# Attention sums of a graph network on Trainium2: blocks of 13 nodes per step instead of 25, six steps' sums copied at once

## The reference

```python
def gatv2_layer(x, src, dst, Wl, bl, Wr, br, att, bias, n_nodes):
    C = att.shape[1]
    xl = (x @ Wl + bl).reshape(n_nodes, H, C)
    xr = (x @ Wr + br).reshape(n_nodes, H, C)
    e = jax.nn.leaky_relu(xl[src] + xr[dst], NEG_SLOPE)
    alpha = jnp.einsum('ehc,hc->eh', e, att)
    m = jax.ops.segment_max(alpha, dst, num_segments=n_nodes)
    m = jnp.where(jnp.isfinite(m), m, 0.0)
    a = jnp.exp(alpha - m[dst])
    denom = jax.ops.segment_sum(a, dst, num_segments=n_nodes)
    a = a / (denom[dst] + 1e-16)
    out = jax.ops.segment_sum(a[:, :, None] * xl[src], dst, num_segments=n_nodes)
    return out.mean(axis=1) + bias
...
h = jax.nn.relu(gatv2_layer(x, src, dst, W1l, b1l, W1r, b1r, att1, bias1, n))
h = jax.nn.relu(gatv2_layer(h, src, dst, W2l, b2l, W2r, b2r, att2, bias2, n))
return h @ Wfc + bfc
```

## Time and profile before

| | us |
|---|---|
| median of 3 runs | 6792.11 (6786.22 to 6797.61) |
| profiled execution | 6792.24 |
| its span | 6790.6 |
| TensorE busy (matmul) | 4317.3 (64%) |
| VectorE busy | 4718.2 (69%) |
| ScalarE busy | 2352.3 (35%) |
| GpSimd busy | 3732.1 (55%) |
| first layer's sums, first to last matmul | 4795.5 to 5106.1 |
| last matmul of the second layer's sums | 6664.5 |

### The profile page before, as it was taken

The page is one execution under the profiler, slowest core; times in us unless marked ns, Lnnn a source line. Parts: engine busy times, 40 slices in busy tenths (PEclk is TensorE's granted clock), DMA queues, the critical chain, the costliest instruction groups (busy, mean ns, idle before and its releaser), DMA issues. The chain is left out here.

```text
span 6790.6 us, 97826 instructions
## 1 busy us (share of the span) xinstructions
PE 4317.3 (64%) x25290; PEld 3565.7 (53%) x25291; DVE 4718.2 (69%) x7252; ACT 2352.3 (35%) x3587; POOL 3732.1 (55%) x4221
## 2 busy tenths in 40 slices
PE   5888889210168846666655656664697666665597
PEld 2788888210058846566653333333696333333496
DVE  4677777688721127777756988887675998887674
ACT  5555555116612216666641112111221112111121
POOL 3677777000200027777754777774655777775453
PEclk9555555555569878888877888887897888888796
DMA  8799898994478753343435777775664777776562
GB/s 325 239 264 261 262 267 259 240 258 156 166 289 304 270 183 113 129 140 113 151 87 131 191 201 202 201 201 141 138 142 123 195 200 202 201 201 165 119 144 63
DMA packets 1471918, 1296.05 MB, mean 191 GB/s; under 512 B 1257959, under 2 KB 1297403, under 8 KB 1458874
## 3 DMA queue, kind: packets, MB, share of 16 engines
q1 hardware_dynamic: 902214, 671.42, 32.9%
q0 software_dynamic: 167008, 441.69, 24.2%
q10 hardware_dynamic: 402580, 181.62, 9.7%
HBM read 942.07 MB, written 351.27 MB: 190 GB/s over the span
## 5 line engine op out<-in xcount | busy, mean ns | idle before, releaser
L2519 POOL DMA_INDIRECT rows_p<-node_rows,stage_i x1632 | 1543.2, 946 | 562.5 <-issue 544.5
L2579 PE MATMUL psZ<-parts_r,hot_t 128*128 x3264 | 1239.1, 535 | 734.5 <-DVE lz L2646 722.8
L2579 PEld LDWEIGHTS psZ<-parts_r,hot_t 128*128 128x128 f32 x3264 | 711.2, 228 | 1261.7 <-issue 1105.4
L731 POOL DMA_INDIRECT rows_s<-hpx,hpST x784 | 739.8, 944 | 264.2 <-issue 243.8
L1972 POOL DMA_INDIRECT both<-table,srcI x784 | 739.8, 944 | 244.4 <-issue 238.6
L2654 DVE TENSOR_TENSOR psZ<-psZ,rows_p 128x1320 f32<-128x1320 f32 x408 | 625.7, 1534 | 227.9 <-DMA rows_p<-node_rows,stage_i 186.0
L749 PE MATMUL psP<-window,pair_hot 128*128 x3136 | 692.4, 413 | 103.4 <-DVE pair_run L828 75.2
L749 PEld LDWEIGHTS psP<-window,pair_hot 128*128 128x128 f32 x3136 | 669.1, 323 | 120.2 <-issue 119.8
L2611 ACT ACTIVATE near<-locs,node_lane 128x1536 bf16<-128x1536 uint8 x136 | 214.2, 1575 | 1490.4 <-DMA locs<-loc_rows 1490.2
L2961 PE MATMUL ps_steps<-A,xs 128*65 128x125 f32 x5184 | 580.5, 272 | 135.2 <-DVE A L2979 92.8
L2646 DVE SCALAR_TENSOR_TENSOR lz<-psZ,att 128x1320 f32<-128x1320 f32 (+2 forms) x428 | 641.8, 1500 | 8.4
(11 more groups left out here) (542 smaller groups left out, 7353.5 us busy)
## 6 DMA issues: line engine op xcount, KB each, us to landing
tile<-adj SPq DMA_DIRECT2D x168, 781.2 KB, 5.1
xs<-x_src SPq DMA_DIRECT2D x432, 128.0 KB, 3.1
x_src<-rows_p SPq DMA_DIRECT2D x204, 256.0 KB, 4.0
hpx<-stage ACTq DMA_DIRECT2D x25, 2048.0 KB, 6.9
window<-hpx SPq DMA_DIRECT2D x196, 256.0 KB
dst_runs<-pair_run SPq DMA_DIRECT2D x28, 1792.0 KB, 7.9
eaT<-in_ea SPq DMA_DIRECT2D x28, 1792.0 KB, 7.0
adj<-tile SPq DMA_DIRECT2D x42, 781.2 KB, 4.8
```

Of the source, the lines that this page charges most:

```text
L731: pool.indirect_dma_start(rows[:, k, j, :], None, g.hpx, bass.IndirectOffsetOnAxis(g.hpST[:, x * K + j:x * K + j + 1], 0)).then_inc(got[k] ...
L2519: pool.indirect_dma_start(rows[:, k, j, :], None, g.node_rows, bass.IndirectOffsetOnAxis(stage[:, k, j:j + 1], 0)).then_inc(got[k], 16)
L2579: last = pe.matmul(psZ[:, n % 2, j, 0:ZH], hot[:, k, col * CE:(col + 1) * CE], parts[:, bass.ds(at[col], 1), :].rearrange("p o c -> p (o c)"),
```

## The change

The block becomes 13 nodes, so that there are 241 blocks (the last one partly beyond the nodes) and 444 places in the table, 37 turns. `A` has 65 columns per step (24 x 65 = 1560 in a half), the mask 24 x 13 = 312, and a step's sum is 65 x 65. Six sums take 390 columns, which fit one bank of PSUM, so that one ScalarE operation copies them where two did. The number of matmuls per step stays at four. Loads of `xs` are as large as before, but there are 444 in place of 324 in each layer. `gat_output` keeps its stride of 125 columns, now written as `NB * H`. The table is made in four groups of 111 steps instead of three of 108. Within a turn the order of the instructions on every engine stays as it was, but for the one copy.

```diff
@@ -36,14 +36,15 @@
 EG = 4
 CW = P * EG
 NC = EP // CW
-WN = NB
-NWIN = N // WN
+WN = 13
+NWIN = -(-N // WN)
+LANES = N // NB
 WC = WN * H
-LP, LQ = 108, 3
+LP, LQ = 111, 4
 LS = LP * LQ
 U = 6
 FP = 16
-assert LS >= NC + NWIN + 1 and LS % (2 * U) == 0 and NC % 2 == 0
+assert LS >= NC + NWIN + 1 and LS % (2 * U) == 0 and NC % 2 == 0 and U * WC <= 512
@@ -2833,7 +2834,7 @@
         A, part = s.sb("A", [P, 2, U * EG, WC]), s.sb("part_w", [D + 1, 2, U * WC])
         hot = s.ps("hotw", [P, 2, U * EG, WN])
-        ps = s.ps("ps_steps", [P, 2, 2, 512])
+        ps = s.ps("ps_steps", [P, 2, 512])
@@ -2842,7 +2843,7 @@
-        slot = lambda k, j: ps[0:D + 1, k, j // 4, (j % 4) * WC:(j % 4 + 1) * WC]
+        slot = lambda k, j: ps[0:D + 1, k, j * WC:(j + 1) * WC]
@@ -2890,8 +2891,7 @@
                     act.wait_ge(stepped[k], i + 2)
                     act.wait_ge(added, i * (2 * U) + (k + 1) * U)
-                    act.activation(part[:, k, 0:4 * WC], ps[0:D + 1, k, 0, 0:4 * WC], ACT.Copy)
-                    act.activation(part[:, k, 4 * WC:U * WC], ps[0:D + 1, k, 1, 0:(U - 4) * WC], ACT.Copy).then_inc(copied, 1)
+                    act.activation(part[:, k, :], ps[0:D + 1, k, 0:U * WC], ACT.Copy).then_inc(copied, 1)
@@ -3025,14 +3025,14 @@
-                        last = pe.matmul(ps[0:NWIN, b % BANKS, h * D:(h + 1) * D], acc[:, b * H + h:NWIN * WC:WC],
+                        last = pe.matmul(ps[0:LANES, b % BANKS, h * D:(h + 1) * D], acc[:, b * H + h:N * H:NB * H],
```

More of the change, by code:

```diff
@@ L3034, in _ @@
                 act.wait_ge(cleared, 1)
-                act.dma_start(flat(den[0:NWIN]), acc[D:D + 1, 0:NWIN * WC].rearrange("o (w f) -> o w f", f=WC)).then_inc(turned, 16)
+                act.dma_start(flat(den[0:LANES]), acc[D:D + 1, 0:N * H].rearrange("o (w f) -> o w f", f=NB * H)).then_inc(turned, 16)
                 act.wait_ge(ready, 1)
@@ L3082, in _ @@
                         v.wait_ge(made, n + 1)
-                        v.tensor_tensor(heads(prod[0:NWIN, n % RING, :]), heads(ps[0:NWIN, n % BANKS, 0:HD]), over(r[0:NWIN, n, :]),
+                        v.tensor_tensor(heads(prod[0:LANES, n % RING, :]), heads(ps[0:LANES, n % BANKS, 0:HD]), over(r[0:LANES, n, :]),
                                         ALU.mult).then_inc(weighed, 1)
```

## The result

The changed kernel takes 7013.2 us, median of 5 runs (7000.3 to 7019.6), against 6792.1 us before (6778.1 to 6798.8, 5 runs): a ratio of 1.0324 with a 95% interval of 1.0312 to 1.0336, 221 us more. The forecast was 6945 us in a range of 6830 to 7015, slower with a chance of 0.92. The sign and the mechanism held; the size was 68 us short, and the time lies at the very upper end of the range.

What follows compares the result with a forecast made beforehand. TensorE and the reload of xs were taken as near-equal bounds. Turns of 10.2 us, 37 instead of 27, gave +149 us for two layers, tables +4.5: +153 on 6792.24, so 6945 us, range 6830 to 7015.

Steps and rivals of the forecast that it cites:

- TensorE and the reload are bounds of nearly the same size: Attention sums before the change: a turn of 11.07 us is 5.8 us of reloading xs plus one burst; two bursts just fill it.
- Burst of 2.9 us at full clock, 60 ns a record: TensorE in the sums: 48 matmul records of 65 columns at 60 ns each; the other end was no gain, 5.2 us.
- Reload unchanged at 5.8 us: Loading xs into a half's single buffer after its burst: SP's four issues and one landing, independent of block width.
- The clock falls in the new pause, mean 0.85: TensorE in the sums: waiting 2.9 us a turn lowers its granted clock to a mean of 0.85.
- Turn of 10.2: One turn of 12 steps in the sums: 5.8 + 2.9 = 8.7 us, divided by 0.85; range 9.4 to 10.6, chance 0.60.
- The rest is no path: VectorE 4.6 us, GpSimd about 9.0, SP 7.1 and DMA 7.0 a turn: none reaches 10.2 us.
- GpSimd's demand of 9.0 in the first turns: GpSimd with the gathers of the first turns: 10.2 us before, less 1.2 for shorter additions, about 9.0 a turn.
- rival A: Sums: TensorE's clock stays full because the pause may split in two; turn 8.7 us, 6836 us in all, chance 0.17.
- Tables +4.5 us, tail -1.1 us: Making the step tables with a fourth group costs 4.5 us (2 to 7); work behind a layer's last burst shrinks 1.1 us.
- The wait before turn 1: Start of each layer's sums: turn 1 is held by loads of weights on SP, which don't change.
- Rival B: Sums: bursts stay 5.2 us, from a 0.50 clock or weight loads no longer hidden; turn 11.0, 7007 us, chance 0.15.
- The clue against it: Layer output's slow matmuls have 125 weight columns against 64 streamed; the changed sums have 65 against 65.

## Why the prediction came out as it did

- *TensorE and the reload are bounds of nearly the same size.* Right. Four buffers alone take 0.7 us from the turn of before, and what is left is two bursts.
- *Burst of 2.9 us at full clock, 60 ns a record.* Right: 3.00 us for 48 records with the last one's 0.22, 59 ns. Of the two rows that it was taken from, the one of 25 columns bounds nothing, since the clock was 0.50 there; the estimate rests on the other. The Trainium skill, "TensorE: Matmul & The Clock Gate", section "Back-to-back issue gap", gives about 81 ns as the sustained spacing of load and matmul pairs at 128 columns. This case's traces don't agree: 125 columns of bf16 ran at 58 ns and 65 columns of f32 at 59.
- *Reload unchanged at 5.8 us.* **This is the term that was mis-sized.** It measured 6.3 to 6.4: from 4992.83 to 4999.12 are 6.29, plus the 0.1 of rest. I read it as four issues and one landing of fixed length, and took the landing's 3.1 us from a kernel whose two halves loaded 5 us apart. With bursts of 2.8 us the second half's loads set out while the first half's are still coming, and the median landing is 3.8; in the kernel of 17 nodes with two buffers, with 3.7 us between the halves, it is 3.4. That they share the DMA engines was in reach: I had put 12 loads at 7.0 us of full DMA work a turn, but used it only as a bound for the whole turn, never for the reload. Half the bytes took 1.3 us off the landing, and an earlier last issue took next to nothing off the reload.
- *The clock falls in the new pause, mean 0.85.* Right in kind: 0.81, and only the first burst of a turn is slow. With useless work in the pause, the turn fell by 1.5 us, which is 0.15 of the 10.2 foreseen. The first burst measured 4.8 us in the mean instead of 4.4. The pause was longer than the 2.9 thought, 3.0 to 4.3 us; that this is why was not tested.
- *Turn of 10.2.* 11.09. Of the 0.9 us between, 0.6 are the reload and 0.3 the clock. Over 35 turns and two layers that is 62 of the 68 us that were missing.
- *The rest is no path.* Right: A measured 1.782 us (1.80 foreseen), the copy 0.492, most additions 0.30 to 0.32, and SP's issues 2.73. GpSimd's demand of 9.0 in the first turns, which spoke against rival A, was put too high: with four buffers and the same gathers those turns take 7.8.
- *Tables +4.5 us, tail -1.1 us.* The tables took 5.9; the last four casts out of PSUM 4.15 where three took 3.04. The tail fell from 4.5 to 3.5 us. The wait before turn 1, taken as unchanged, grew by 1.8 and 1.4 us in the two layers.
- *Rival B at 7007 us* has nearly the right time, and a turn of 11.0, by the wrong mechanism. Its bursts of 5.2 us were not there: the second burst of a turn took 3.0 to 3.4 us, at full clock or nearly so. The clue against it, in the earlier trace rows, was rightly read.
- *Rival A* needed the pause to split in two. It never did: the second burst followed directly on the first in every turn from turn 2 on, as the prediction had said against it.

## What to carry to other kernels

Before making a step cheaper and having more of them, find what a step costs that doesn't shrink with it. Here each step brought the same 128 KB through the DMA engines and the turn waited for it, so the number of steps was the price and their width nearly free. A reload chain has a part that is bytes on shared engines: when the work between two reloads shrinks, they overlap and each gets longer. And a pause of TensorE can cost twice, as here, once as the pause and once as the slow burst behind it; a third and fourth buffer took nearly all of both away (7.46 us a turn, clock 0.99).

## What the runs showed of the hardware

- Three f32 matmuls of 512 columns a turn that nobody reads made the kernel faster, from a turn of 11.1 to 9.6 us, since the granted clock stayed at 1.00 instead of 0.81.
- Behind pauses of 3.0 to 4.3 us the first burst ran at the lower clock for most of its time in every one of 70 turns (4.3 to 5.5 us where 3.0 is full speed; mean clock 0.61 and 0.65 in two of them); behind pauses of 2.0 to 3.0 us, in the kernel of 17 nodes, in 16 of 60. With 13 nodes and four buffers it was slow in 8 of 70, behind pauses of 1.3 to 2.4 us.
- An f32 record of 65 weights and 65 columns runs at 59 ns at full clock, 0.9 ns a column as the 125 columns of before (108 ns): the weight load of 65 columns adds nothing that shows.
- The loads of xs, in packets of 256 bytes, ran at 218 GB/s over 130 us with four buffers, and at 231 over the 3.7 us of a pause. 64 KB instead of 128 KB a load brought the median landing from 3.8 to 2.0 us and the median issue from 543 to 373 ns.
- The attention's edge stage moved 158 GB/s on the two chips where the kernel before takes 7725 and 7769 us, and 199 where it takes 6792, while a turn of the sums took the same within 0.1 us.
